# Attention with one score pass a head pair: maximum as the exponential's bias, probabilities transposed by DMA

## The reference, cut to what matters

```python
x = x + tanh(g_xattn[0]) * xattn(_layernorm(x), ctx_1024, ...)   # x: (8, 256, 128), ctx: (8, 512, 128)
x = x + tanh(g_ffn[0]) * ffn(_layernorm(x), gate_w, w1, w2)      # top-1 of 8 experts, 160 places each

# xattn: 16 heads of 64
q = (layernorm(x) * ln_gamma + ln_beta) @ w_q                    # 256 queries a batch
k, v = split(context @ w_kv)                                     # 512 keys a batch
scores = einsum('bqhd,bkhd->bhqk', q * 64 ** -0.5, k)
attn = softmax(scores, axis=-1)
out = (einsum('bhqk,bkhd->bqhd', attn, v) @ w_out + b_out) * tanh(gate[0])
```

## Time and profile before

| | us |
|---|---|
| median of 3 runs | 590.01 (590.0 to 590.87) |
| the profiled execution, its own time | 591.27 |
| its span, first to last instruction | 589.4 |
| busy: PE / PEld | 510.6 / 422.9 |
| busy: DVE / ACT / POOL | 411.6 / 359.9 / 327.5 |

### The profile page before, as it was taken

One profiled execution on the slowest core, in us unless ns is written; L12 is line 12 of the kernel. 1 busy time (PEld: TensorE's weight loads), 2 busy tenths in 40 slices (PEclk: granted clock), 3 DMA queues, 4 the chain that ended last, 5 costly groups with the idle time before them and its releaser, 6 DMA issues.

```text
span 589.4 us, 15522 instructions
## 1 busy us (share of the span) xinstructions
PE 510.6 (87%) x6476; PEld 422.9 (72%) x6476; DVE 411.6 (70%) x762; ACT 359.9 (61%) x483; POOL 327.5 (56%) x209
## 2 busy tenths in 40 slices
PE   5789999998898999998898989998898999986294
PEld 3577878776786778776786768776786778775194
DVE  5887786777957776777857786777867775884112
ACT  5667775776656665676656665676656765662041
POOL 4655664555655565465655565465645565564115
PEclk9999999999999989999999999999999999998588
DMA  7800000600000000000000000000000000000201
GB/s 206 281 2 21 1 3 6 166 2 11 11 10 20 2 19 2 28 3 3 18 11 19 3 17 3 28 2 2 14 11 1 2 7 3 10 1 13 85 10 42
DMA packets 19541, 16.18 MB, mean 27 GB/s; under 512 B 2163, under 2 KB 16931, under 8 KB 19472
## 3 DMA queue, kind: packets, MB, share of 16 engines
q1 hardware_dynamic: 18096, 11.88, 6.9%
q0 software_dynamic: 1376, 3.30, 1.5%
HBM read 10.83 MB, written 5.14 MB: 27 GB/s over the span
## 4 chain that ended last, share of the span: by engine, by line
PE 59%; DVE 24%; ACT 7%; issue 7%; DMA 2%; POOL 1%; POOLq 0%; SPq 0%; DVEq 0%
DVE MX L720 7%; PE psAB L926 6%; PE psEF L989 6%; DVE VL L710 5%; PE psO L1051 4%; PE psO L1053 4%; PE psX L1110 4%; PE psO L1052 4%; PE psCD L1030 4%; PE psAB L928 4%; PE psAB L927 4%; ACT VH L562 3%; PE psCD L1025 3%; DVE HL L704 2%; ACT HL L551 2%
## 5 line engine op out<-in xcount | busy, mean ns | idle before, releaser
L495 POOL TENSOR_TENSOR PARTS<-P,PARTS 128x1024 f16<-128x1024 f32 x128 | 274.2, 2145 | 191.5 <-DVE PARTS L728 146.9
L720 DVE TENSOR_REDUCE MX<-psEF 128x2 f32<-128x1024 f32 x128 | 156.3, 1221 | 0.8 <-PE psEF L989 0.4
L1051 PE MATMUL psO<-VH,PARTS 128*128 128x65 f16 x1024 | 100.6, 195 | 0.2 <-DVE winners L794 0.2
L1052 PE MATMUL psO<-VL,PARTS 128*128 128x64 f16 x1024 | 99.9, 193 | 0.0
L1053 PE MATMUL psO<-VH,PARTS 128*128 128x65 f16 x1024 | 99.7, 194 | 0.0
L704 DVE TENSOR_TENSOR HL<-psAB,HL 128x768 fp32r<-128x768 f32 x63 | 60.3, 958 | 53.9 <-ACT HL L551 53.9
L587 ACT ACTIVATE P<-psAB,lift 128x1024 f32<-128x1024 f32 x64 | 71.3, 1114 | 42.3 <-PE psAB L1030 39.2
L1051 PEld LDWEIGHTS psO<-VH,PARTS 128*128 128x128 f16 x1024 | 92.6, 98 | 3.3 <-DVE winners L794 0.3
L1052 PEld LDWEIGHTS psO<-VL,PARTS 128*128 128x128 f16 x1024 | 93.5, 99 | 0.0
L1053 PEld LDWEIGHTS psO<-VH,PARTS 128*128 128x128 f16 x1024 | 93.5, 97 | 0.0
L989 PE MATMUL psEF<-HL 64*128 64x512 f32 x256 | 63.9, 495 | 33.7 <-DVE MX L720 32.3
(11 more groups left out here) (179 smaller groups left out, 899.9 us busy)
## 6 DMA issues: line engine op xcount, KB each, us to landing
ctx_raw<-in_ctx_dram SPq DMA_DIRECT2D x8, 256.0 KB, 2.9
w1s<-in_L_ffn_w_dram SPq DMA_DIRECT2D x8, 256.0 KB, 5.2
w2s<-in_L_ffn_w_dram SPq DMA_DIRECT2D x8, 256.0 KB, 4.7
experts_table<-zeros POOLq DMA_DIRECT2D x2, 645.0 KB
PARTS<-experts_table SPq DMA_DIRECT2D x2, 516.0 KB, 4.3
wraw<-in_L_xattn_w_kv_dram SPq DMA_DIRECT2D x4, 256.0 KB, 4.6
out_dram<-row SPq DMA_DIRECT2D x8, 128.0 KB, 1.8
X<-in_x_dram SPq DMA_DIRECT2D x1, 896.0 KB, 8.3
```

Source lines behind the costliest of these rows:

```text
L495: pool.tensor_tensor(PLO[:, par, :, cols], P32[:, par, :, cols], PHI[:, par, :, cols], ALU.subtract).then_inc(plo_done, 1)
L720: dve.tensor_reduce(maxima, psEF2, AX.X, ALU.max, negate=True).then_inc(max_done, 1)
L1051: pe.matmul(psO[:, g:g + DH + 1], phi, VH[:, kt, head, 0:DH + 1], start=first_, stop=False)
L1052: pe.matmul(psO[:, g:g + DH], phi, VL[:, kt, head, :], start=False, stop=False)
```

## The change

The maximum pass, its transposes and the matmuls with ones are gone. `scores` now writes queries on the partitions and 512 keys along the row: `psAB` holds query half 0 (`qt` 0) of both heads, `psCD` half 1. `row_max` reads the scores themselves, and a small VectorE operation, SCALE times the negated maximum plus LIFT, makes the bias `NB` (L731 of the changed kernel), which the exponentials take; there are four of 512 columns a pair instead of two of 1024. Since values still want keys on the partitions, SyncE transposes the parts by DMA from `PARTS` into `PT`: four transfers a pair of 128 x 1024 float16 (256 KB), the two high parts as soon as they are cast, the low ones as soon as GpSimd has subtracted. Values of a pair come two slots later instead of one. K, Q, V and x projections now share `psEF`, and wait for each other's eviction there; `psAB` and `psCD` serve the scores alone. On ScalarE the cast of the second high part moves behind V's high part. Tokens go to slot 5, token moments to 4, the projection to 3.

```diff
-        PROJECT_STEP = 2
-        CTX_STEP = KT - 1
+        PROJECT_STEP = 3
+        CTX_STEP = 1
+        VALUES_BEHIND = 2
...
-        MOMENTS_STEP, TOK_STEP, TOKT_STEP, LOGITS_STEP, RANKS_STEP = 3, 4, 5, 6, 7
+        MOMENTS_STEP, TOK_STEP, TOKT_STEP, LOGITS_STEP, RANKS_STEP = 4, 5, 5, 6, 7
...
+            def transpose_part(j, qt, part):
+
+                par = j % 2
+                if part == 0:
+                    sp.wait_ge(phi_done[qt], j + 1)
+                    if j >= 2 and qt == 0:
+                        sp.wait_ge(pv_done, j - 1)
+                else:
+                    sp.wait_ge(plo_done, 2 * j + qt + 1)
+                done = lo_in[qt][par] if part else hi_in[qt][par]
+                sp.dma_start_transpose(PT[:, par, qt, part].rearrange("p h k n -> p (h k) n"),
+                                       PARTS[:, par, qt, part]).then_inc(done, 16)
...
+                    for part in range(2):
+                        for qt in range(QT):
+                            transpose_part(j, qt, part)
...
-                            pool.wait_ge(pv_done, j - 1)
...
+                            pool.wait_ge(lo_in[qt][par], transposed_value(j - 2))
...
+                act.wait_ge(bias_done, 2 * j + qt + 1)
+                for h in range(2):
+                    last = act.activation(P32[:, par, qt, SK * h:SK * h + SK], score_bank(qt)[:, SK * h:SK * h + SK],
+                                          ACT.Exp, bias=NB[:, par, qt, h:h + 1], scale=SCALE)
...
+                dve.wait_ge(score_psum, 2 * j + qt + 1)
+                dve.tensor_reduce(MX[:, par, qt, :], score_bank(qt)[:].rearrange("p (h n) -> p h n", h=2), AX.X, ALU.max,
+                                  negate=True).then_inc(max_done, 1)
+                dve.wait_ge(max_done, 2 * j + qt + 1)
+                dve.tensor_scalar(NB[:, par, qt, :], MX[:, par, qt, :], SCALE, LIFT, ALU.mult, ALU.add)\
+                   .then_inc(bias_done, 1)
...
+                    pe.wait_ge(kq_lo_done, j)
+                    for free_when in ef_free:
+                        pe.wait_ge(*free_when)
...
+                    pe.wait_ge(kq_lo_done, min(behind + 1, B * PAIRS))
+                    ef_free.append(v_free)
...
+                if j:
+                    pe.wait_ge(exp_done, 2 * j - 2 + qt + 1)
+                for k, q in ((H_KHI, H_QHI), (H_KLO, H_QHI), (H_KHI, H_QLO)):
+                    for h in range(2):
+                        rows = slice(64 * h, 64 * h + 64)
+                        last = pe.matmul(score_bank(qt)[:, SK * h:SK * h + SK], hl[rows, q + P * qt:q + P * qt + P],
+                                         hl[rows, k:k + SK], start=(q == H_QHI and k == H_KHI), stop=(q == H_QLO))
```

More of the change, by code:

```diff
@@ L873, in batch @@
                         ctxt_lo(b + 1)
+                    if hp == PROJECT_STEP and not is_first(b):
+                        add_attention(b - 1)
+                    if hp == MOMENTS_STEP and not is_first(b):
+                        token_moments(b - 1)
+                    if hp == TOK_STEP and not is_first(b):
+                        tokens(b - 1)
+                    if v_group(b, hp):
+                        v_lo(*v_group(b, hp))
                     if hp == LOGITS_STEP and not is_first(b):
@@ L980, in max_scores @@
                 if qt == 0:
-                    pe.wait_ge(kq_hi_done, j + 1)
-                    if j:
-                        pe.wait_ge(mrow_done, j)
-                else:
-                    pe.wait_ge(max_done, 2 * j + 1)
-                for h in range(2):
-                    rows = slice(64 * h, 64 * h + 64)
-                    last = pe.matmul(psEF[:, 512 * h:512 * h + SK], hl[rows, H_QHI + P * qt:H_QHI + P * qt + P],
-                                     hl[rows, H_KHI:H_KHI + SK], start=True, stop=True)
@@ L991, in max_scores @@
-                last.then_inc(smax_psum, 1)
-            def max_transpose(b, hp):
-                j = b * PAIRS + hp
-                pe.wait_ge(max_done, 2 * j + 2)
-                for qt in range(QT):
-                    last = pe.transpose(psEF[:, P * qt:P * qt + P], MX[:, hp % 2, qt, :], ident[:])
-                last.then_inc(mt_psum, 1)
-            def scores(b, hp, c):
-                j = b * PAIRS + hp
-                hl = HL[:, hp % 2, :]
-                if c == 0:
-                    pe.wait_ge(mrow_done, j + 1)
-                    pe.wait_ge(kq_lo_done, min(j + 2, B * PAIRS))
-                    if j == 0:
-                        pe.wait_ge(row_consts, 4)
-                    if j + 1 >= B * PAIRS:
-                        pe.wait_ge(exp_done, 2 * j - 1)
-                elif j == 0:
-                    pass
-                elif v_group(*back(b, hp, 1)):
-                    vb, half, kt = v_group(*back(b, hp, 1))
-                    pe.wait_ge(v_lo_done, vb * 2 * KT + half * KT + kt + 1)
-                else:
-                    pe.wait_ge(exp_done, 2 * j)
-                heads = [(slice(64 * h, 64 * h + 64), score_bank(c)[:, 512 * h:512 * h + 512]) for h in range(2)]
-                for rows, dst in heads:
-                    both = NM[rows, :].unsqueeze(1).to_broadcast([64, 2, SQ])
-                    pe.matmul(dst.rearrange("p (i n) -> p i n", i=2), ones_r[rows, :], both, start=True, stop=False)
-                for i in range(2):
-                    kt = 2 * c + i
-                    for k, q in ((H_KHI, H_QHI), (H_KHI, H_QLO), (H_KLO, H_QHI)):
-                        for rows, dst in heads:
-                            last = pe.matmul(dst[:, SQ * i:SQ * i + SQ], hl[rows, k + P * kt:k + P * kt + P],
-                                             hl[rows, q:q + SQ], start=False, stop=(i == 1 and k == H_KLO))
@@ L1175, in batch @@
                         project(b - 1)
+                    if hp == CTX_STEP and not is_last(b):
+                        ctx_transposes(b + 1)
+                    if j >= VALUES_BEHIND:
+                        values(*back(b, hp, VALUES_BEHIND))
                     if hp == TOKT_STEP and not is_first(b):
@@ L1178, in batch @@
                     if v_group(b, hp):
-                        if j == 0:
-                            pe.wait_ge(w_lo_rest_done, 3)
-                        v_project(*v_group(b, hp), after_exp=2 * j + 2)
+                        v_project(*v_group(b, hp), behind=j + AHEAD)
                     if hp == X_STEP and not is_last(b):
-                        x_transposes(b + 1)
-                    if hp == CTX_STEP and not is_last(b):
-                        ctx_transposes(b + 1)
+                        x_transposes(b + 1, j + AHEAD)
+                    if hp == LOGITS_STEP and not is_first(b):
+                        logits(b - 1, min(j + AHEAD, B * PAIRS - 1))
                 if is_last(b):
-                    pe.wait_ge(route, (B - 2) * ROUTE + 7)
+                    values(b, PAIRS - 2)
+                    pe.wait_ge(kq_lo_done, B * PAIRS)
+                    for free_when in ef_free:
+                        pe.wait_ge(*free_when)
+                    o_transposes(b, 2, psEF[:, 512:1024])
                     project_last(b, range(PAIRS - 2))
```

255 lines of the change are left out of this document (108 added, 147 removed).

## The result

The changed kernel takes **649.29 us** in the median (648.42 to 650.48, 4 runs) against 590.0 (588.98 to 590.87): a ratio of 1.1007, interval 1.0982 to 1.1032, so 59 us or 10% slower. The profiled execution took 650.48 us, with a span of 648.7.

The account below looks back on a forecast made before the run. A ring of steps, no engine alone, was taken to bound each slot. A batch of 71.8 us, 5.3 more, gave 37 over seven periods: 591.3 - 3 + 37 + 5 = 630.3, less 1.3, so 629 us; range 575 to 675.

Parts of the forecast that it names:

- The bias is stopped by 1.3 us in every slot: VectorE's first bias waits for GpSimd's second subtraction, ending at 3.3 instead of 2.05 us, in each slot.
- Slot 3 at 8.6: TensorE's own list of work is longer than the ring there: 8.6 us, so 1.2 over a plain slot.
- Slot 1 at 10.1: Plain slot of 7.4 plus 2.7 us: L687 twice (1.8 and 0.33) and the context's low part (0.6).
- Slot 5 at 11.1: Tokens wait for GpSimd's first subtraction and their transposes stand ahead of V's projection: 3.7 us over a plain slot.
- A ring without the stop, 6.1: A plain slot's chain of waits would take 6.1 us if GpSimd did not stop the bias.
- Slot 4 as a plain slot of 7.4: Slot 4 was given no batch extra, only the plain ring of 7.4 us including the bias stop.
- Slot 6 at 9.3: L794 takes 2.08 us instead of 0.17 while GpSimd's subtraction runs: 1.9 over a plain slot of 7.4.
- The clock, 1.0 us a batch: TensorE at 1.2 GHz after idling lengthens V's projection by 0.5 us, taken twice a batch; between 0 and 4.
- DMA transposes at 1.3 us each, hidden: Transposes take 5.2 us of a 9.0 slot, hidden; as a rival, they set the pace from 2.25 each, chance 0.10.
- Ends, +2: Outside the steady batches, the kernel's start was to take 3 us less and its end 5 more.
- The free bias: Rival: the bias slips past GpSimd or is not stopped, slot 6.1 us, kernel 519, up to 540; chance 0.14.
- Half and half: Rival: the bias stop is there, but batch extras of 11.6 us come out at 5; kernel 583; chance 0.08.

Follow-up runs that it names:

- f_warm: Changed kernel with 6 filler matmuls of 248 columns a slot on TensorE between the scores and K's projection: 651.58 us, ratio 1.104.
- f_order_tok: Changed kernel with only the token moments and tokens moved ahead of the first high part on VectorE: 592.34 us, ratio 1.0046.
- e_double: Changed kernel with a second DMA transpose, of zeros, behind each; the queue also waits each slot for the added ones of the slot before: 928.29 us.
- e_nobias: Changed kernel without its bias operation, gamma and beta scaled once at the start, the constant 7 left out: 614.47 us, ratio 1.0381.
- e_order: Changed kernel with all VectorE batch work (statistics and normalisation of x, token moments, tokens) moved ahead of the first high part: 588.28 us, ratio 0.9953.

## Why the prediction was right, and where its steps were not

The direction, the time (649 in a range of 575 to 675) and the mechanism hold: small operations of VectorE between SBUF operands are stopped by GpSimd's subtraction, and a slot is a ring in which that counts. That GpSimd is what stops them is read from the ends that coincide and from the same operations running free where no subtraction runs; no run takes the subtraction away and leaves VectorE's order as it is. The predicted 629 was 20 us short, and that it came so near is in part luck. The eight predicted slots add up to 70.8 us, the measured ones to 75.1; but three were 3.2 too long in sum and four 7.5 too short, and where the prediction has the same 1.3 us of stop in every slot, the trace has it in few, and longer stops and a lower clock in others. By its steps:

- **The bias is stopped by 1.3 us in every slot: wrong in how often.** In a steady batch it is stopped for 1.1 us in two slots of eight (3 and 4), for 0.8 in a third (6) and for 0.2 in a fourth (1); its mean is 0.418 us, where 0.8 was named as the mark. In the others VectorE came behind the subtraction. The term was 8 x 1.3 = 10.4 us a batch. The stops come to 4.0 a batch (32 us in eight), and removing the operation gave 4.4 (35 us in eight). That the two agree is no proof, as removing it also took away its free time and half of the stops of x's normalisation.
- **Slot 3 at 8.6: right** (8.6), with TensorE busy throughout; its terms as given add up to 8.5. **Slot 1 at 10.1: the number is right** (9.9), by luck: the normalisation was stopped twice, not once, and the bias for 0.2, not 1.3. **Slot 5 at 11.1: near** (10.6), also in part by luck: the tokens were stopped for 1.5 where the sum has 2.15, no bias was stopped, and the slot ran at a clock of 0.66, which the sum doesn't have. (Its terms as given add up to 11.3.) **Slot 0 at 9.5: too long** (7.0): no bias stop there.
- **A ring without the stop, 6.1: right.** Slot 2, in which VectorE has no stop and no batch work, takes 6.25 at a clock of 1.00 in `f_warm` and in `f_order_tok`.
- **Slot 4 as a plain slot of 7.4: the step that failed most** (11.2). I had the stop for L673, L687, L794 and the tokens, but gave slot 4 no extra at all: its token moments end in a two-column tensor_scalar (L784) of the very form of L673, ahead of V's low part. **Slot 7** the same with L828 (9.2, not 7.4), stopped 1.8 us in seven of its eight instances; the sum left it out, although L816, its form before, had taken 1.97 once. **Slot 6 at 9.3** came out at 10.4.
- **The clock, 1.0 us a batch: too small.** 171 us of the span ran at half clock, where the sum had two projections of V in a batch. Slot 2 alone lost 1.8 to 1.9 us a batch by it (8.2 at 0.62, 6.2 at 1.00), behind slot 1, in which TensorE had been busy for little over half. The term was missed where it mattered: a whole slot of TensorE's work slowed down, not one step of the ring.
- **DMA transposes at 1.3 us each, hidden: right.** Where one follows another they go at 1.35 in the median, 5.4 us a slot, and with half of them gone the time is the same. The bound from which they would decide, 9.0 / 4 = 2.25 each, was not tested as it stands; `e_double` halves the room instead, and adds a wait. (In that rival the kernel at 2.4 each would take 675 us by its own formula, not 660.) The Trainium skill has two figures that were named there. The estimate from the first, 1.0 us a transfer (DMA: Bandwidth & Descriptors, Latency and other measured facts), is low by 0.35 against the pace here. The second is 1,309 ns for one 128 x 128 block (VectorE: DVE Perf Modes, The three transpose paths); here whole transfers of eight blocks follow each other at about that pace, each landing 3.2 us after its issue.
- **Ends, +2: not settled.** The spans differ by 59.3 us, and a steady batch by 8.5 (75.0 against 66.5), which in seven is 60. Seven intervals between every eighth cast of V, though, are 47 to 65 us longer than before, depending on the cast with which one starts, as the first and the last batch are not steady. That leaves anything from -6 to +12 for the ends.
- **Rivals.** The free bias (519) is what `e_nobias` made true as far as the bias goes, and it gave 614: the other stops and the ring still stood. "Half and half" (583) is near what `e_order` measures with its batch work out of GpSimd's way (588), but not by that rival's sum: the bias's stops rose there to 55 us.

What the diff had done, and I had read only in part, is to move the token moments and tokens from behind V's low part to ahead of it. Moved further ahead, in front of the first high part, 57 of the 59 us are gone, with the new scores, the bias and the transposes all in place. Of the 10.1 us that a batch loses by this move, 3.3 are these groups' own stops (slots 4 and 5), 1.5 one stop less in slot 1, 1.9 the clock in slot 2, 0.8 lie in slot 6 and 0.1 in slot 3; the 2.4 left in slot 5 were not divided between the clock and the earlier tokens.

## What to carry to other kernels

Where two engines stop each other, count the stops by place, not by operation: a two-column operation costs the rest of the other engine's instruction, and its price can be multiplied if the next thing on that engine is what a third one waits for. Ask too whether the third engine, having waited, comes back slower: read the granted clock of the slot behind a long one, as a total hides what one slot gains and another loses. Put small operations of that kind where the other engine is known to be idle, behind a step that starts it, and keep operations that aren't stopped for the rest. And when a bank is moved to open a ring, first list who holds the new bank.

## What the runs showed of the hardware that was not expected

- Which operations are stopped depends on their kind, not only on where their operands lie. I took, in the changed kernel, those that began at least 0.1 us after the start and 0.6 before the end of a subtraction. Stopped, every one: tensor_scalar (63 of them, L684, L698, L731, L784, L789, L828) and, with two SBUF inputs, L806, L811 and L823 (one of each). Free, every one: what reads PSUM (L721, L728, L753, 45 of them), and also, between SBUF operands, the statistics (L676, 12, at their 0.28), the aggregation (L679, 14) and the tensor_reduce of slot 7 (L827, 7, at 0.17), as here, where GpSimd's pair of subtractions runs from 233.11 to 237.35:

```profile
233.11 4.24 POOL L512 TENSOR_TENSOR PARTS<-P,PARTS 128x1024 f16<-128x1024 f32 x2 [1.10 <-DVE PARTS L740]
233.49 0.48 DVE L676 BATCH_NORM_STATS2 stats<-X 128x6 f32<-128x128 f32 x2
233.89 0.30 DVE L679 BATCH_NORM_AGGREGATE mv<-stats 128x2 f32<-128x6 f32 x2
234.22 1.06 DVE L684 TENSOR_SCALAR vv<-mv 128x2 f32<-128x2 f32 x1
```

  The Trainium skill (SBUF — State Buffer, SBUF: two separate sides) has the pair of ports that VectorE and GpSimd share as an exclusive lock, held for a whole instruction, for VectorE operations with two SBUF inputs or in a two-port mode. The stopped operations with two SBUF inputs agree with that, with GpSimd as the one that holds it. Whether the tensor_scalars ran in such a mode no row shows, and none here shows GpSimd waiting.
- One waiting operation of VectorE gets through where one subtraction ends and the next begins, even with no gap: L684 above ends at 235.28, the first subtraction by its own record at 235.26. A second one waiting behind it is held through the next subtraction too (3.4 us over free for two instructions that take 0.6), unless there is a gap: one of 0.20 us was enough.
- The granted clock costs what TensorE's place in the slot makes it cost: 1.8 us in slot 2 between 0.63 and 1.00, nothing in slot 7 between 0.81 and 1.00.
- A DMA transpose of 256 KB from SBUF to SBUF is taken every 1.35 us by one queue (1.27 to 1.51 where one follows another) and lands after 3.2 us in the median (3.4 with twice as many), so two or three are in flight; twice as many on the same queue kept that pace (1.36 to 1.38) and so took it twice the time.
